# Gate logits taken straight into rows in both expert stages, and the second stage's normalisation done by ScalarE

## The reference, cut to what matters

```python
# layer 1 (x: normalised rows, context: other rows)
logits = einsum('bsd,de->bse', context, Wg) + bg
scores_topk, idx_topk = top_k(logits, 2)
combine = sum(one_hot(idx_topk, 8) * softmax(scores_topk)[..., None], axis=-2)
h = relu(einsum('bsd,edf->bsef', x, W1) + b1)
out = einsum('bsed,bse->bsd', einsum('bsef,efd->bsed', h, W2) + b2, combine)
# layer 2 (xt: normalised rows of the sum so far)
gates = softmax(xt @ wg, axis=-1)
expert_idx = argmax(gates, axis=-1)
pos = place of a row within its expert; keep = pos < 512
out = (relu(disp @ w1 + b1) @ w2 + b2)[slot] * gate_val
```

## Time and profile before

| | us |
|---|---|
| median of three runs | 1555.9 (1555.59 to 1556.89) |
| the profiled execution, its own time | 1555.87 |
| its span, first to last instruction | 1554.2 |
| PE busy | 1264.6 (81%) |
| DVE busy | 1154.8 (74%) |
| ACT busy | 836.4 (54%) |
| POOL busy | 470.6 (30%) |

### The profile page before, as it was taken

The page is one execution under the profiler, slowest core; times in us unless marked ns, Lnnn a source line. Parts: engine busy times, 40 slices in busy tenths (PEclk is TensorE's granted clock), DMA queues, the critical chain, the costliest instruction groups (busy, mean ns, idle before and its releaser), DMA issues. The chain is left out here.

```text
span 1554.2 us, 31503 instructions
## 1 busy us (share of the span) xinstructions
PE 1264.6 (81%) x10394; PEld 1028.0 (66%) x10395; DVE 1154.8 (74%) x2027; ACT 836.4 (54%) x1273; POOL 470.6 (30%) x487
## 2 busy tenths in 40 slices
PE   6999999999999573999936899999997599930087
PEld 3468888888889532898825888888886254310076
DVE  3869865655556377996528999999997686999754
ACT  4866633333333151663314667767663667897664
POOL 3234755555553303445222222322323000000000
PEclk9999999999999885999965799999987699975599
DMA  9887633232332284773143010000000001454111
GB/s 320 313 268 218 155 52 54 44 52 45 51 46 37 29 277 127 215 195 54 25 112 101 21 28 24 23 27 25 22 15 6 36 1 61 166 207 146 70 55 55
DMA packets 108486, 146.77 MB, mean 94 GB/s; under 512 B 17072, under 2 KB 84400, under 8 KB 106608
## 3 DMA queue, kind: packets, MB, share of 16 engines
q1 hardware_dynamic: 87280, 116.31, 22.7%
q0 software_dynamic: 21120, 29.30, 11.3%
HBM read 92.35 MB, written 53.23 MB: 94 GB/s over the span
## 5 line engine op out<-in xcount | busy, mean ns | idle before, releaser
L734 ACT ACTIVATE top_x_all<-top_h_ps,top_b1T 128x256 f32<-128x256 f32 x440 | 181.2, 474 | 287.3 <-PE top_h_ps L580 287.3
L578 PE MATMUL top_h_ps<-top_xT_hi,top_w_hi 128*128 128x256 f16 x880 | 240.7, 273 | 1.3 <-DVE top_xT_lo L921 0.8
L579 PE MATMUL top_h_ps<-top_xT_lo,top_w_hi 128*128 128x256 f16 x880 | 240.6, 273 | 0.0
L580 PE MATMUL top_h_ps<-top_xT_hi,top_w_lo 128*128 128x256 f16 x880 | 240.6, 273 | 0.0
L596 PE MATMUL top_y_ps<-top_w_hi,top_x_all 128*128 x880 | 239.9, 273 | 0.5 <-DVE top_x_all L934 0.3
L597 PE MATMUL top_y_ps<-top_w_lo,top_x_all 128*128 x880 | 239.9, 273 | 0.0
L598 PE MATMUL top_y_ps<-top_w_hi,top_x_all 128*128 x880 | 239.9, 273 | 0.0
L932 DVE CAST top_x_all<-top_x_all 128x512 f16<-128x512 f32 x220 | 96.5, 439 | 141.5 <-ACT top_x_all L734 141.4
L934 DVE TENSOR_TENSOR top_x_all<-top_x_all 128x512 f16<-128x512 f32 x220 | 153.1, 696 | 7.6
L387 POOL DMA_INDIRECT x_sum<-top_x_all,top_row_of_slot x54 | 92.5, 1712 | 171.9 <-DVE top_x_all L946 144.6
L1749 PE MATMUL ffn_ps<-ffn_dT_hi,ffn_yT 128*128 128x256 f16 x192 | 53.5, 278 | 107.2 <-DVE ffn_yT L2033 107.2
(11 more groups left out here) (321 smaller groups left out, 3169.3 us busy)
## 6 DMA issues: line engine op xcount, KB each, us to landing
top_staged<-in_L_xattn_W SPq DMA_DIRECT2D x32, 512.0 KB, 6.3
top_staged<-in_L_ffn_w SPq DMA_DIRECT2D x32, 512.0 KB, 6.4
up_raw<-ffn_u_all SPq DMA_DIRECT2D x48, 256.0 KB, 2.0
ffn_yT<-up_raw SPq DMA_DIRECT2D x12, 1024.0 KB, 4.8
kv_rows<-top_w_lo SPq DMA_DIRECT2D x32, 256.0 KB, 4.0
attn_kv_in<-kv_rows SPq DMA_DIRECT2D x32, 256.0 KB, 2.6
top_w_lo<-in_ctx SPq DMA_DIRECT2D x4, 1024.0 KB, 9.7
top_x_all<-in_x SPq DMA_DIRECT2D x4, 1024.0 KB, 12.0
```

Of the source, the lines that this page charges most:

```text
L578: nc.tensor.matmul(out, hi, xT_hi[p][:, c, :], start=(c == 0), stop=False)
L579: nc.tensor.matmul(out, hi, xT_lo[p][:, c, :], start=False, stop=False)
L580: last = nc.tensor.matmul(out, lo, xT_hi[p][:, c, :], start=False, stop=(c == DC - 1))
L734: last = nc.scalar.activation(h32[:, fc * R:(fc + 1) * R], h_ps[:, b, q * R:(q + 1) * R], ACT.Relu, bias=b1T[:, bass.ds(e * FC + fc, 1)], ...
```

## The change

In both stages the gate product changes sides: for each tile of 128 rows the transposed rows are stationary (128 columns) and `wg_sb` is moving (8 columns), so the result lies in rows at once. `lgT`, ACT's `logits_copy` and PE's `logits_back` go, and the routing waits for `s_lg`. In top1, ACT normalises in place of DVE, with the code of top2: its square root now stands behind all eight gate copies, its first quarter ahead of the exponential, the other three behind it, and `split_hi(act, 0)` behind these.

```diff
             def gate_logits(g):
                 pe.wait_ge(s_trc, g + 1)
-                if g >= 2:
-                    pe.wait_ge(s_lgc, g - 1)
-                for c in range(DC):
-                    mm = nc.tensor.matmul(xT_ps[g % 2][0:E, :], wg_sb[:, c, :], gateT[g % 2][:, c, :], start=(c == 0), stop=(c == DC - 1))
-                mm.then_inc(s_lg, 1)
-
-            def logits_back(g):
-                pe.wait_ge(s_lgc, g + 1)
                 for k in range(GC):
                     t = g * GC + k
-                    mm = nc.tensor.transpose(lg[:, t * E:(t + 1) * E], lgT[g % 2][:, k * P:(k + 1) * P], ident[0:E, 0:E])
-                mm.then_inc(s_lt, 1)
+                    for c in range(DC):
+                        mm = nc.tensor.matmul(lg[:, t * E:(t + 1) * E], gateT[g % 2][:, c, k * P:(k + 1) * P], wg_sb[:, c, :],
+                                              start=(c == 0), stop=(c == DC - 1), skip_group_check=True)
+                mm.then_inc(s_lg, 1)
...
             for g in range(GROUPS):
                 gate_copy(g)
-                if g > 0:
-                    logits_copy(g - 1)
                 if kv is not None and g in (2, 3):
                     kv_weights_hi(g - 2)
-                if gate_source is None and g == 3:
-                    act.wait_ge(s_var, 1)
-                    nc.scalar.activation(rstd[:], rtmp[:], ACT.Sqrt).then_inc(s_root, 1)
-            if gate_source is not None:
-                act.wait_ge(s_var, 1)
-                nc.scalar.activation(rstd[:], rtmp[:], ACT.Sqrt).then_inc(s_root, 1)
-            logits_copy(GROUPS - 1)
+            act.wait_ge(s_var, 1)
+            nc.scalar.activation(rstd[:], rtmp[:], ACT.Sqrt).then_inc(s_root, 1)
...
-            if gate_source is not None:
-                act.wait_ge(s_scales, 1)
-                normalise(0)
-                kv_copies(0, 4)
-            else:
-                split_hi(act, 0)
+            act.wait_ge(s_scales, 1)
+            normalise(0)
+            kv_copies(0, 4)
             act.wait_ge(s_diff, 1)
...
             else:
                 nc.scalar.activation(work, work, ACT.Exp).then_inc(s_exp, 1)
+                for q in range(1, 4):
+                    normalise(q)
+                split_hi(act, 0)
...
-            if gate_source is not None:
-                V.scalar_tensor_tensor(shift[:], mean_var[:, :, 0], -1.0, rstd[:], ALU.mult, ALU.mult).then_inc(s_scales, 1)
-            else:
-                for t in range(T):
-                    if t % GC == 0:
-                        dve.wait_ge(s_tr, t // GC + 1)
-                    mm = V.tensor_scalar(x_all[:, t, :], x_all[:, t, :], mean_var[:, t, 0:1], rstd[:, t:t + 1],
-                                         ALU.subtract, ALU.mult)
-                    if (t + 1) % (T // 4) == 0:
-                        mm.then_inc(s_normed, 1)
+            V.scalar_tensor_tensor(shift[:], mean_var[:, :, 0], -1.0, rstd[:], ALU.mult, ALU.mult).then_inc(s_scales, 1)
```

More of the change, by code:

```diff
@@ L172, in experts @@
         gateT = [late[:, p * DC * GN:(p + 1) * DC * GN].rearrange("p (c t) -> p c t", c=DC) for p in range(2)]
-        lgT = [late[0:E, (2 * DC + p) * GN:(2 * DC + p + 1) * GN] for p in range(2)]
         if gate_source is not None:
@@ L257, in experts @@
         s_tr = sem("gate_transposed"); s_trc = sem("gateT_ready")
-        s_lg = sem("logitsT_product"); s_lgc = sem("logitsT_ready"); s_lt = sem("logits_transposed")
+        s_lg = sem("logits_product")
         s_wstored = sem("weights_stored"); s_wts = sem("weights_by_token")
@@ L523, in _ @@
                     gate_transposes(g + 1)
-                if g > 0:
-                    logits_back(g - 1)
                 gate_logits(g)
@@ L528, in _ @@
                     kv_weights(g)
-            logits_back(GROUPS - 1)
             kv_products(0, 4)
@@ L667, in kv_copies @@
                             act.wait_ge(s_ctx["lo"], GROUPS)
-                            act.wait_ge(s_lt, GROUPS)
+                            act.wait_ge(s_lg, GROUPS)
                         if b >= STORES:
@@ L809, in _ @@
             dve.wait_ge(s_const, 10)
-            dve.wait_ge(s_lt, GROUPS)
+            dve.wait_ge(s_lg, GROUPS)
             lg = y_ps[1][:, 0:T * E].rearrange("p (t e) -> p t e", e=E)
```

## The result

The change makes the kernel slower: 1581.5 us median of four runs (1576.3 to 1586.2) against 1556.4 of the kernel before in the same comparison, a ratio of 1.0157 (95% interval 1.0128 to 1.0186). A second comparison of the same two kernels gave 1.0144 (1.0119 to 1.0168). The forecast was 1580 with a range from 1562 to 1585. The profiled execution of the changed kernel took 1586.2 us, with a span of 1583.8 against 1554.2.

The account below looks back on a forecast made before the run. PE was taken to bound the gate loops and to be busy nearly throughout the main loops; narrow products at half clock add 9.5 us in top2, and with late stores 14.6 in top1: 1555.87 + 9.5 + 14.6 = 1580.0 us, range 1562 to 1585.

Parts of the forecast that it names:

- Which clock: Gate loops of both setups: PE's clock falls within the first groups and stays at 1.2 GHz until wide products come; 0.70.
- the arrival at half: Top2's gate loop: PE already arrives at half clock behind its wait for the keys' weights, eight transposes taking 1.91 us.
- Price of a group: Gate loops: one narrow group takes 2.8 us at full clock, 0.35 less than now, or 5.15 at half, 2.0 more.
- The first rival: Gate loops: the clock falls late or comes back between, about half of fourteen groups at full; 1566 us, chance 0.12.
- Top2: First setup: routing starts at 54.4 instead of 46.11, +8.3; with keys and DVE waits +9.5 us in all (6 to 11).
- DVE waits that vanish: Top2: of PE's 1.6 us of waits for DVE about 1.3 us vanish.
- The keys' term: Top2 behind the gate loop: the keys' first four products at first still run at half, +2.5 us (0 to 3.5).
- Top1, the products: Second setup's gate loop: logits come late at half clock, routing starts at 588.1 in place of 577.63.
- Top1, the stores: Second setup: gather waits for stores behind ACT's late normalising, 5.5 + 12.1 + 0.4 + 2.7 + 7.2 us after routing, at 616.0.
- The rival with stores that are hidden: Both setups: full clock, top1's stores landing before the table, so both gain in full; 1549.5 us, chance 0.07.
- Gather to first product: Top1's end: gather to first expert product takes 10 us instead of 12.2 (8 to 13).
- Whatever a setup gains or loses moves the rest of the run by the same amount: Main loops behind both setups: PE is busy nearly throughout, so nothing else moves.

Follow-up runs that it names:

- the kernel with the products alone: Narrow gate products in both setups against the kernel before, DVE still normalising in top1; ratio 1.0102, profiled span 1575.6 us.
- the third profile: The changed kernel profiled a third time without an edit; 942.6 us from the second setup's first product to the end.
- the kernel with this part alone: Second setup's rows normalised on ACT against the kernel before, wide gate products kept; ratio 1.003, profiled execution 1562.1 us.

## Why the prediction was right

**Which clock.** Right, and it decided the sign. The prediction read one stretch of the attention where PE was busy for all of 3.40 us and the clock fell behind it, and took the new loop to be of that kind. In the changed kernel PE is busy for 20.00 of 20.00 us at the low clock:

```profile
560.00:580.00 20.00, 20.00 (x98) 20.00 (x97) 10.54 (x57) 4.09 (x4) 0.00 (x0) 0.50 0.59 197
```

How it came about differs by run. I had the clock fall within the first groups. In the first two profiles of the changed kernel it was never up in either gate loop: the first sixteen narrow records, from 14.42, already take 3.42 us. In the third, and in the kernel with the products alone, the first two groups of top2 ran at full. The first of them in the latter:

```profile
14.58 1.95 PE L487 MATMUL top_y_ps<-top_wg_sb,top_w_lo 128*128 128x8 f32 x16
```

PE then waited for DVE (4.67 us here, 5.24 in the third profile), came back at half and stayed there, which is the arrival at half that the prediction has for top2. In the second setup of the third profile the clock came up in the first group and fell within the second, with no wait between.

The Trainium skill ("TensorE: Matmul & The Clock Gate", section "HAM oscillation — how this bites in real kernels") ties the loss of the clock to gaps in PE's work. The kernel with the last four groups narrow does not agree: in its first setup the clock fell within the second narrow group, and PE had had no gap since 24.31. In the second setup of the changed kernel PE came to the loop at half, behind waits of 17.10 and 2.31 us, and did not get the clock in 40 us without a gap.

One stretch of the attention was little to go by. With a product added the same code ran at either clock, and in the first setup of the kernel with the last two groups narrow the clock held through 3.7 us of narrow products. That nearly every group ran at half is in part luck.

**Price of a group.** At half 5.01 us, where I had 5.15: a hair too high. The first rival's price does not follow from its own terms: seven of fourteen groups at 2.35 us less give 1563.5 and not 1566; nothing else rests on it. The 1.80 for sixteen records at full is 1.79 in the kernel with a product added.

**Top2.** Routing at 54.65, +8.5 where the sum had +8.3. Two errors cancel in that: the stretch of six groups of products and four of transposes began at 27.65 and not at 26.9, since the groups ahead of it ran at half too, and it took 26.7 us (to 54.38) and not 27.4. Then +2.5 for the keys' first products at half and -1.3 for DVE waits that vanish came to +1.2; measured is +0.4 (8.9 at the first product, 8.5 at routing). In all +8.9 for +9.5. The keys' term was the one too large: from the first of these products to the 24th it took 4.97 us before (45.93 to 50.90) and 6.44 after (54.38 to 60.82), so 1.5 and not 2.5. In the third profile it took 7.48.

**Top1, the products.** All eight groups at half; in two other profiles one of them and part of a second ran at full (40.8 and 41.2 in the second column). I had taken one at full, routing at 588.1 and +10.5; measured +11.3.

**Top1, the stores.** Expected 5.5 + 12.1 + 10.3 = 27.9 us from routing to the gather; measured 5.4 + 11.9 + 10.1 = 27.3, and 27.9 in the kernel with this part alone. The rival with stores that are hidden has fallen with it: even at the full clock they bind by 6.3 us. That the small stores and not only the rows are what is waited for is shown by their move, which took 3.7 us off.

**Gather to first product.** This term was mis-sized: I took 10 us for 12.2. All twelve profiles have 11.6 to 12.6. Where both tiles' rows land together, as in the changed kernel, it is 11.6 to 11.8, so 0.6 is gained and not 2.2. No run shows what makes them land together. This is the larger part of the 1.9 us by which top1 came out longer than the sum (16.5 for 14.6).

**What was not in the sum.** "Whatever a setup gains or loses moves the rest of the run by the same amount" fits the medians (+25.1 us), not single executions. Behind the setups the first profile of the changed kernel has 4.6 us more than that of before, most of it at the end of the attention, the second 0.7 and the third none. By the setups alone the ratio should be 25.4 / 1556, 1.6%; both comparisons hold that in their intervals.

**What stays open.** What exactly the clock depends on is not settled. The runs show that a loop of narrow products with a stationary load each loses it or does not get it, that a wide product in every group may or may not hold it, and that the wide ones of the kernel before held it, once it was up, in all three profiles in which they stood alone. A version with the narrow products at full clock in both setups was not found.

## What to carry to other kernels

Before a wide product is replaced by many narrow ones, ask what TensorE's clock will be with them: price both at half and at full, and look for a stretch of the trace in which PE already does the like, even if it is in another stage. Work taken off an engine that waits anyway is worth nothing, and its new place can cost: ask which stores stand behind it in SP's queue and who waits for the last of them. When the profile of a changed kernel differs by more than the edit explains, profile both kernels again before explaining the rest.

## What the runs showed that I had not expected

- **Busy is not fast.** PE stayed at 1.2 GHz for the whole gate loop of the second stage with PE and its loads busy all the time, 20.00 of 20.00 us. In the kernel with a product added PE was busy at 1.2 GHz for 26.5 of 26.5 us, then the clock came up in the middle of a loop that does the same in each group.
- **The record of the clock can be missing.** Two profiles of one kernel, the changed one, over the same stretch of the first gate loop, first run and third:

```profile
30.00:54.00 24.00, 24.00 (x116) 24.00 (x116) 13.14 (x65) 10.52 (x14) 10.60 (x5) 1.00 0.78 271
```
```profile
30.00:54.00 24.00, 24.00 (x116) 24.00 (x117) 13.13 (x65) 10.53 (x14) 10.28 (x5) 0.50 0.77 271
```

  The same 116 records take the same 24.00 us, one time with PEclk 1.00 and one time with 0.50. The durations tell the clock there (3.42 us for sixteen records), and the first reading is wrong; so is the 1.00 in the first window of this part.
- **The clock at the end of the attention varies from run to run** by 4.8 us of PE time (13.05 to 17.89), and the whole by some 4 us, in kernels that are the same there.
